# A metaformer block on one core: experts' outputs laid side by side with both image halves on the partitions, and a last stage that adds on GpSimd in place of folding matmuls

## The reference, cut

```python
topk_s, topk_i = jax.lax.top_k(scores, TOP_K)
w = jax.nn.softmax(topk_s, axis=-1)
out = jnp.zeros_like(x)
for ei in range(NUM_EXPERTS):
    g = jnp.where(topk_i == ei, w, 0.0).sum(-1)
    hh = jax.nn.gelu(x @ W1[ei] + b1[ei], approximate=False)
    out = out + g[..., None] * (hh @ W2[ei] + b2[ei])
```

## Time and profile before

| | us |
|---|---|
| three runs | 4731.93, 4735.66, 4740.96; median 4735.66 |
| the profiled execution | 4737.77, its span 4736.0 |
| edge stage, from the first gather to the last scatter | 1431 to 4308 |
| last stage, first load issued to the end | 4449 to 4736 |
| busy over the span | PE 3866.3 (82%), POOL 2844.5 (60%), DVE 2657.0 (56%), ACT 942.1 (20%) |

### The profile page before, as it was taken

How to read it: one execution, slowest core, us unless ns; L and a number is a source line. 1 busy time by engine, 2 the same in 40 slices (tenths; PEclk the granted TensorE clock), 3 DMA queues, 4 the chain that set the end, 5 groups by cost and what they waited for, 6 DMA issues and landing times. The chain is left out here.

```text
span 4736.0 us, 62817 instructions
## 1 busy us (share of the span) xinstructions
PE 3866.3 (82%) x21121; PEld 2690.0 (57%) x21121; DVE 2657.0 (56%) x3261; ACT 942.1 (20%) x2069; POOL 2844.5 (60%) x2881
## 2 busy tenths in 40 slices
PE   4785333799948999999999999999999999661499
PEld 1453223577736666666666666666666667561122
DVE  7779999667644444444444444444444444447666
ACT  0110000000012333332333333333333333110000
POOL 2001888766626777777777777777777777771000
PEclk8897555788867888988888988889888888776699
DMA  1232111788862111111111111111111111682498
GB/s 48 69 96 74 49 47 35 85 107 102 102 107 49 34 35 34 36 35 35 35 35 35 35 35 35 35 33 37 32 38 33 35 35 34 10 10 3 137 289 247
DMA packets 323403, 284.04 MB, mean 60 GB/s; under 512 B 201074, under 2 KB 279154, under 8 KB 322804
## 3 DMA queue, kind: packets, MB, share of 16 engines
q1 hardware_dynamic: 213732, 200.98, 19.9%
q0 software_dynamic: 91008, 30.58, 11.5%
q10 hardware_dynamic: 18576, 51.39, 2.8%
HBM read 160.41 MB, written 122.31 MB: 60 GB/s over the span
## 5 line engine op out<-in xcount | busy, mean ns | idle before, releaser
L1074 POOL DMA_INDIRECT gath<-tab_d,src_no x2288 | 2158.9, 944 | 775.8 <-issue 696.9
L446 POOL DMA_INDIRECT edge_d<-run_slots,slots x544 | 657.2, 1208 | 662.8 <-ACT run_slots L636 502.2
L1204 PEld LDWEIGHTS C<-spread,lo_hot 128*128 128x128 f32 x4576 | 848.1, 244 | 331.3 <-DVE spread L1359 173.7
L1204 PE MATMUL C<-spread,lo_hot 128*128 128x160 f32 x4576 | 920.2, 370 | 139.4 <-DVE spread L1359 139.1
L1193 PEld LDWEIGHTS C<-dst_rows,lo_hot_t 128*128 128x128 f32 x4576 | 586.7, 208 | 91.1 <-issue 78.3
L1371 DVE TENSOR_TENSOR acc<-acc,C 128x160 f32 x572 | 183.5, 321 | 796.3 <-PE C L1204 746.8
L1193 PE MATMUL C<-dst_rows,lo_hot_t 128*128 128x32 f32 x4576 | 603.9, 289 | 11.2 <-ACT lo_hot_t L1092 11.2
L1214 PE MATMUL A<-T,w1s 64*128 64x392 f32 x1024 | 533.8, 605 | 0.0
L1097 ACT ACTIVATE hid<-A,b1s 128x392 f32<-128x392 f32 x512 | 300.6, 587 | 1078.9 <-PE A L1214 1078.9
L557 PE MATMUL C<-wide_rec,hot_lo 128*128 128x136 f16 x2048 | 266.8, 305 | 296.9 <-DVE wide_rec L814 296.9
L1225 PE MATMUL A<-hid,w2s 128*64 128x392 f32 x1024 | 456.3, 528 | 0.0
(11 more groups left out here) (263 smaller groups left out, 3195.6 us busy)
## 6 DMA issues: line engine op xcount, KB each, us to landing
mlp_d<-mlp ACTq DMA_DIRECT2D x128, 392.0 KB
mlp<-mlp_d SPq DMA_DIRECT2D x64, 784.0 KB, 4.7
gath<-tab_d,src_no POOLq DMA_INDIRECT x2288
pixels<-in_x SPq DMA_DIRECT2D x32, 392.0 KB, 8.1
src<-in_x SPq DMA_DIRECT2D x32, 392.0 KB, 9.2
T<-t_d SPq DMA_DIRECT2D x128, 98.0 KB
X<-x_d SPq DMA_DIRECT2D x64, 196.0 KB, 5.4
out<-X SPq DMA_DIRECT2D x128, 98.0 KB, 2.6
```

Source lines behind the costliest of these rows:

```text
L446: pool.indirect_dma_start(edge_d, bass.IndirectOffsetOnAxis(ap=slots[:, k, c:c + 1], axis=0), run_slots[:, k, c * RUN:(c + 1) * RUN, :].re ...
L1074: pool.indirect_dma_start(gath[:, g % BUFS, j, :], None, tab_d, bass.IndirectOffsetOnAxis(ap=src_no[:, t:t + 1], axis=0)).then_inc(gathere ...
L1204: mm = pe.matmul(C[:, bank, at:at + HI * VALS], lo_hot[:, k, u * U + j, :], spread[:, u * U + j].rearrange("p h v -> p (h v)"), start=(j = ...
```

## The change

The experts' outputs are stored side by side: `mlp_d[m]` is 128 partitions (both halves) by four experts by 392. `down` writes expert e of half h to partitions `h * 64` on of bank A3, and ScalarE evicts each expert by itself (`expert_out`), 64 partitions at a time, four times a group where there were two. The biases `b2s` have a column for each expert. `pick` has 24 rows and 128 columns: rows 0 to 11 spread the upper half's gates over channels 0 to 63, rows 12 to 23 the lower half's over 64 to 127; six selections build it. The gates are loaded twice, the second time shifted by half an image (1568 pixels, 12 pieces and 32 pixels), in three transfers where there was one.

In the last stage TensorE spreads four gates of a chunk with four matmuls into the four banks of A or C in turn. VectorE multiplies all four experts at once (128 x 1568) and adds experts 0, 1 to 2, 3 (128 x 784). GpSimd adds the two remaining parts and then the residual, each 128 x 392. No fold is left.

```diff
-        mlp_d = dram("mlp_d", [B * CHUNKS, 2, P, 2, CHUNK])
+        mlp_d = dram("mlp_d", [B * CHUNKS, P, EXPERTS, CHUNK])
...
-        b2s = sb("b2s", [P, 2])
-        pick = sb("pick", [3 * EXPERTS, EXPERTS, CH], BF16)
+        b2s = sb("b2s", [P, EXPERTS])
+        pick = sb("pick", [2 * 3 * EXPERTS, EXPERTS, P], BF16)
...
-                for r in range(3):
-                    link(pool, pool.affine_select(out=pick[:], in_=pick[:], compare_op=ALU.not_equal, fill=1.0, base=-r * EXPERTS,
-                                                  pattern=[[-1, EXPERTS], [0, CH]], channel_multiplier=1), step)
+                for h in range(2):
+                    mine = pick[:, :, h * CH:(h + 1) * CH]
+                    for r in range(3):
+                        link(pool, pool.affine_select(out=mine, in_=mine, compare_op=ALU.not_equal, fill=1.0, base=-(h * 3 + r) * EXPERTS,
+                                                      pattern=[[-1, EXPERTS], [0, CH]], channel_multiplier=1), step)
...
-                def pair_out(m, h, j):
-
-                    if j == 0 and not (isinstance(m, int) and m == 0):
+                def expert_out(m, h, e):
+
+                    v = (m * 2 + h) * EXPERTS + e
+                    a = slice(h * CH, (h + 1) * CH)
+                    if e == 0 and not (isinstance(m, int) and m == 0):
                         act.wait_ge(mlp_stored[h], m * 16)
-                    act.wait_ge(s["pair_done"], (m * 2 + h) * 2 + j + 1)
-                    act.activation(mlp[:, h, j, :], A[:, 3, 0:CHUNK], ACT.Identity, bias=b2s[:, j:j + 1]).then_inc(s["pair_out"], 1)
-                    if j == 1:
-                        act.wait_ge(s["pair_out"], (m * 2 + h) * 2 + 2)
+                    act.wait_ge(s["expert_done"], v + 1)
+                    act.activation(mlp[a, e, :], A[a, 3, 0:CHUNK], ACT.Identity, bias=b2s[a, e:e + 1]).then_inc(s["expert_out"], 1)
+                    if e == EXPERTS - 1:
+                        act.wait_ge(s["expert_out"], (m * 2 + h) * EXPERTS + EXPERTS)
                         act.sem_inc(s["act_turns2"], 1)
-                        act.dma_start(mlp_d[m, h].rearrange("p j n -> p (j n)"), mlp[:, h].rearrange("p j n -> p (j n)")).then_inc(mlp_stored[h], 16)
+                        act.dma_start(mlp_d[m, a].rearrange("p e n -> p (e n)"), mlp[a].rearrange("p e n -> p (e n)")).then_inc(mlp_stored[h], 16)
...
                     if with_mlp:
+                        expert_out(m, h, 0)
                         gelu(m, h, 1)
-                        pair_out(m, h, 0)
+                        expert_out(m, h, 1)
                         gelu(m, h, 2)
                     if left >= 2:
                         turned_copy(g + 2, 0)
                     if with_mlp:
+                        expert_out(m, h, 2)
                         gelu(m, h, 3)
                     if left >= 2:
                         turned_copy(g + 2, 1)
                     if with_mlp:
-                        pair_out(m, h, 1)
+                        expert_out(m, h, 3)
...
                 def down(m, h, e):
-                    v = m * 2 + h
-                    pe.wait_ge(s["gelu_ready"], v * EXPERTS + e + 1)
-                    if e % 2 == 0 and not (isinstance(m, int) and m == 0 and h == 0 and e == 0):
-                        pe.wait_ge(s["pair_out"], v * 2 + e // 2)
-                    a = slice(e % 2 * CH, (e % 2 + 1) * CH)
-                    mm = pe.matmul(A[a, 3, 0:CHUNK], w2s[:, e, :], hid[:], start=True, stop=True)
-                    if e % 2:
-                        mm.then_inc(s["pair_done"], 1)
+                    v = (m * 2 + h) * EXPERTS + e
+                    pe.wait_ge(s["gelu_ready"], v + 1)
+                    if not (isinstance(m, int) and m == 0 and h == 0 and e == 0):
+                        pe.wait_ge(s["expert_out"], v)
+                    pe.matmul(A[h * CH:(h + 1) * CH, 3, 0:CHUNK], w2s[:, e, :], hid[:], start=True, stop=True).then_inc(s["expert_done"], 1)
...
-            gate_t = tb("gate_t", [3 * EXPERTS, 2, PAIR_Q, P], BF16)
+            gate_t = tb("gate_t", [2 * 3 * EXPERTS, 2, PAIR_Q, P], BF16)
             NBUF, AHEAD = 8, 6
-            mlp = tb("mlp3", [P, NBUF, 2, 2, CHUNK])
+            mlp = tb("mlp3", [P, NBUF, EXPERTS, CHUNK])
             X1 = tb("X1", [P, NBUF, CHUNK])
-            gated = tb("gated", [P, 4, CHUNK])
-            s = sems("gate_ready gated_ready folded summed3 sp_turns3 gate_loaded0 gate_loaded1")
+            gated = tb("gated", [P, 2, EXPERTS, CHUNK])
+            pairs = tb("pairs", [P, 2, 2, CHUNK])
+            four = tb("four", [P, 2, CHUNK])
...
-                    sp.dma_start(mlp[:, k], mlp_d[n].rearrange("s p j n -> p s j n")).then_inc(chunk_in[k], 16)
+                    sp.dma_start(mlp[:, k], mlp_d[n]).then_inc(chunk_in[k], 16)
...
                 def load_gates(pair, half):
-                    sp.dma_start(gate_t[:, half], gate_d.rearrange("k q e l -> e (k q) l")[:, bass.ds(pair * PAIR_Q, PAIR_Q), :]).then_inc(s[f"gate_loaded{half}"], 16)
+                    rows = gate_d.rearrange("k q e l -> e (k q) l")
+                    low, high = gate_t[0:3 * EXPERTS, half], gate_t[3 * EXPERTS:2 * 3 * EXPERTS, half].rearrange("e q l -> e (q l)")
+                    first, whole = P - SHIFT_L, PAIR_Q - SHIFT_Q - 1
+                    sp.dma_start(low, rows[:, bass.ds(pair * PAIR_Q, PAIR_Q), :]).then_inc(s[f"gate_loaded{half}"], 16)
+                    sp.dma_start(high[:, 0:first], rows[:, bass.ds(pair * PAIR_Q + SHIFT_Q, 1), SHIFT_L:P].rearrange("e q l -> e (q l)")).then_inc(s[f"gate_loaded{half}"], 16)
+                    sp.dma_start(high[:, first:first + whole * P].rearrange("e (q l) -> e q l", l=P),
+                                 rows[:, bass.ds(pair * PAIR_Q + SHIFT_Q + 1, whole), :]).then_inc(s[f"gate_loaded{half}"], 16)
...
+            def gates_of(t):
+
+                return (A, C)[t % 2][:, :, 0:CHUNK]
+
             @block.tensor
             def _(pe):
-                def spread_gates(r, t, h, j, first):
-
...
+                def spread_gates(r, t, first):
+
+                    n = (t % PER) // CHUNKS * HGT * WID + t % CHUNKS * CHUNK
+                    if t % PER == 0:
+                        pe.wait_ge(s[f"gate_loaded{t // PER}"], (r + 1) * 48)
+                    if t >= 2 or not first:
+                        pe.wait_ge(s["gated_ready"], r * STEPS + t - 1)
+                    for e in range(EXPERTS):
+                        mm = pe.matmul(gates_of(t)[:, e], pick[:, e, :], gate_t[:, t // PER].rearrange("e q l -> e (q l)")[:, n:n + CHUNK], start=True, stop=True)
+                    mm.then_inc(s["gate_ready"], 1)
+
+                for t in range(STEPS):
+                    spread_gates(0, t, True)
                 with pe.Fori(1, ROUNDS) as r:
-                    round_of(r, False)
+                    for t in range(STEPS):
+                        spread_gates(r, t, False)
+
+            @block.gpsimd
+            def _(pool):
+                def add_up(r, t, first):
+                    n = r * STEPS + t
+                    hold(pool, s["paired"], n + 1, s["pool_turns3"])
+                    pool.tensor_tensor(four[:, t % 2], pairs[:, t % 2, 0], pairs[:, t % 2, 1], ALU.add).then_inc(s["added"], 1)
+                    pool.wait_ge(s["added"], n + 1)
+                    pool.tensor_tensor(X1[:, t % NBUF], X1[:, t % NBUF], four[:, t % 2], ALU.add).then_inc(s["summed3"], 1)
+
+                for t in range(STEPS):
+                    add_up(0, t, True)
+                with pool.Fori(1, ROUNDS) as r:
+                    for t in range(STEPS):
+                        add_up(r, t, False)
 
             @block.vector
             def _(dve):
-                def add_x1(r, t):
...
-                def round_of(r, first):
...
+                def weigh_and_pair(r, t, first):
+                    n = r * STEPS + t
+                    dve.wait_ge(chunk_in[t % NBUF], (r * (STEPS // NBUF) + t // NBUF + 1) * 32)
+                    dve.wait_ge(s["gate_ready"], n + 1)
+                    if t >= 2 or not first:
+                        dve.wait_ge(s["paired"], n - 1)
+                        dve.wait_ge(s["added"], n - 1)
+                    dve.tensor_tensor(gated[:, t % 2], mlp[:, t % NBUF], gates_of(t), ALU.mult).then_inc(s["gated_ready"], 1)
+                    dve.wait_ge(s["gated_ready"], n + 1)
+                    dve.tensor_tensor(pairs[:, t % 2], gated[:, t % 2, 0:2], gated[:, t % 2, 2:4], ALU.add).then_inc(s["paired"], 1)
+
+                for t in range(STEPS):
+                    weigh_and_pair(0, t, True)
+                with dve.Fori(1, ROUNDS) as r:
                     for t in range(STEPS):
...
+                        weigh_and_pair(r, t, False)
```

48 lines of the change are left out of this document (5 added, 43 removed).

## The result

The changed kernel took 4687.74 us, median of 4 runs (4679.31 to 4694.19), beside 4738.31 us for the kernel before, median of 4 (4731.93 to 4742.18). The ratio is 0.9894, with an interval of 0.9874 to 0.9914: faster by 50.6 us where 68 were forecast, inside the range of 4646 to 4712. A second set of runs of both kernels gave 0.9878 [0.985, 0.9906]. The profiled execution of the changed kernel is the fastest of its four, 4679.31 us by its own clock, with a span of 4677.6, so 9.6 us above the forecast end of 4668.0.

A forecast was written before the change was run, and what follows sets the result against it. GpSimd's gathers bound the edge stage, a chain through TensorE's folds the last. Without folds, transfers at 3.35 us a chunk save 68 us there, other stages nothing: 4735.7 - 68 = 4667.7, called 4668 us, range 4646 to 4712.

The forecast's parts named there:

- The edge stage and the setup: Ahead of the last stage: 256 added ScalarE evictions cost 0 to +10 us, three more selections at most 1 us.
- VectorE's product: Last stage: one VectorE product of 1568 elements a chunk, priced at 1.79 us.
- the two gaps: Last stage, VectorE: two gaps of 0.04 us a chunk beside product and pair addition, 2.76 us becoming 2.84 us.
- GpSimd's addition: Last stage: each of GpSimd's two 392-element additions a chunk takes 0.85 us, bounds 0.50 and 1.25.
- its sign: Changed profile's last stage: GpSimd's addition 0.8 to 0.9 us, or near 1.8 where it waited for a pair addition.
- the engines' sum: Last stage, engines alone: first product at 4456.7, 64 x 2.97 = 190.1 us, then additions and store, ending at 4652.
- The exclusion: Last stage: VectorE's pair addition from SBUF and GpSimd's additions wait each other out, 2.97 us a chunk against 2.84.
- the rival by which the product is shut out too: Last stage: GpSimd's additions also block VectorE's product, 4.76 us a chunk, end at 4768; chance 0.05.
- The rival of slow GpSimd: Last stage: GpSimd additions of 1.25 us, 3.77 us a chunk, end at 4704 (4685 to 4712); chance 0.13.
- the likeliest case: Last stage: transfers set the pace at 3.25 to 3.6 us a chunk, total 4661 to 4684; chance 0.56.
- the fast end: Last stage transfers: 3.27 us a chunk at the loads' rate, against 3.54 at the mixed one; 3.35 taken.
- the transfers' sum: Last stage: data from 4450.2, 64 x 3.35 = 214.4 us of transfers, about 3.4 us at the end: 4668.0.

The follow-up runs named there:

- the first four experiments: Changed kernel without most large loads, with transfers alone, half the product in PSUM, all additions on VectorE: 53.0, 41.0, 46.4 and 6.7 us faster than before.
- the second experiment: Changed kernel with only one 128 x 392 VectorE multiplication a chunk and no GpSimd work in the last stage, all transfers kept: 3.346 us a chunk.
- the repeat: The changed kernel run once more, unaltered, in another set: median 4680.6 us, ratio 0.989 to the kernel before, 3.332 us a chunk.

## Why the prediction was right, and by how much it was not

**The edge stage and the setup** cost nothing, as forecast: 2856 us of gathers for 2855, and no more with ScalarE's added evictions tripled. The selections are one row of six, 6.54 us against the 9.2 I had allowed. That holds where GpSimd sets the pace; by the totals of the first four experiments it may not hold on a chip where it does not.

**TensorE** drops out: its four matmuls take 1.48 us a chunk (1.3 to 1.5 forecast), at half the clock.

**VectorE's product** is 1.78 us (1.79 forecast). One of the two gaps was wrong in sign: products start 0.08 us before the pair addition ahead of them ends, while the pair addition starts 0.04 us after its product; and the first distance, before GpSimd has begun, is 2.71 us where I had 2.84.

**GpSimd's addition** is 1.01 us where I took 0.85, inside my bounds of 0.50 and 1.25 (the row of 512 elements gives 1.23) but above the 0.8 to 0.9 that I named as its sign. It is the most mis-sized price of the engines' sum.

**The exclusion** is there, and only as far as I had it: the pair addition with both operands in SBUF goes from 0.97 to 1.38 us beside GpSimd, and not at all with one operand in PSUM (970 ns in every form); the product keeps its 1.78 us beside GpSimd, so the rival by which the product is shut out too, 4.76 us a chunk, falls. The Trainium skill (SBUF — State Buffer, Who interferes with whom) states it as a rule: a VectorE instruction with two SBUF inputs and a GpSimd instruction that reads SBUF contend, one with a single SBUF input outside the two-port modes does not. The traces agree on all three operations: 1.38 us for the pair addition from SBUF, 0.97 with one operand in PSUM, 1.78 for the product. Not all of the wait is lost: the pair addition ends 0.83 us after GpSimd, where 0.10 + 0.97 were in my sum. So the loop is 0.19 + 1.01 + 0.08 + 1.01 + 0.83 = 3.12 us for 0.14 + 0.85 + 0.06 + 0.85 + 0.10 + 0.97 = 2.97. The rival of slow GpSimd needed 1.25 us an addition and a chunk of 3.77; GpSimd lay nearer to my value than to it.

**The transfers** set the pace in the mean, as the likeliest case said: 3.35 forecast, 3.343 and 3.332 in the change, 3.346 with the engines' work gone. Of its parts, 2.98 us for the bytes was 2.95, and the reason that I gave for the fast end, queues as full as in the first microseconds, is what the second experiment shows. The gates were priced a quarter too low, 0.29 us a chunk for 0.39 (85.75 pieces, not the 85.5 of my text, makes no difference). These two make 3.27, and I went up to 3.35 for stores mixed in among the loads, which cost nothing: 408 GB/s with them, 404 without. So the agreement to 0.01 us is partly luck, since a surcharge without a cause stood in for the part of the gates' cost that I had missed. Why a gate load costs so much no run shows.

The Trainium skill's planning figure of about 358 GB/s (SBUF — State Buffer, Summary: rules for kernel authors) would have given, as an estimate, 3.65 us; the measured 3.343 decides against it, for here the queues moved 408 GB/s of loads and stores together between gate loads, and 368 with them.

**The sum** is where most of the 9.6 us went. I let 64 chunks of 3.35 run from the first data and added 3.4 us. The trace has 63 distances of 3.343 between products, with 8.0 us ahead of them (I had counted 1.3 us to the first data and one chunk of 3.35, 4.65) and 8.8 us behind (3.4): +3.3, +5.4 and -0.4 are 8.3 us, and the stage's start lay 1.3 us later than before, together the 9.6. The start was in my text, a first product at 4456.7 in the engines' sum, and did not enter the transfers' sum. The tail is a product of 1.78 us, a pair addition of 1.39, two of GpSimd's at 1.01 and 3.3 us from the sum to the end of its store; the additions and the store alone are 6.7 us, and I had 3.4.

The other 8 us between the profiled run and the median are not the change's. From its first issue the last stage took 227.4 us in the first profile and 226.5 in the repeat, 60 us less than before's 287.1 and 287.0; the ratio's interval allows 41 to 60 us, the second one's 44 to 71, and the first gather alone wanders by 25 us. A saving of 60 us fits both; the medians' 50.6 and 52.6 us lie below it, within the scatter of the stages ahead.

## What to carry to other kernels

When a fold or reduction leaves the critical path, the next limits can lie within a few tenths of a microsecond of each other: here 3.35 for transfers, 3.11 for the engines with the exclusion, 2.77 without. Lifting the exclusion alone gave nothing once and 3 us of the stage the second time; lifting it and the transfers' limit, at the price of rounding the experts' outputs to bf16, took 36 us from the stage. Price a pipelined stage as fill, plus (n - 1) periods, plus drain, each from its own rows; the period was right to 0.01 us, partly by luck, and the ends cost 9. And where two SBUF operands meet on VectorE beside a busy GpSimd, leaving one of them in PSUM removes the wait at the price of splitting one instruction.
